# The first 21 of 98 destination blocks of a graph network leave the dense count matrices and take row gathers with one-hot products

## The reference

```python
deg_out = segment_sum(ones, src, N); deg_in = segment_sum(ones, dst, N)
dout, din = maximum(deg_out, 1) ** -0.5, maximum(deg_in, 1) ** -0.5
def conv(x, W, b):                       # run twice, with W1, b1 and W2, b2
    m = (x * dout[:, None])[src]         # one row for each edge
    return segment_sum(m, dst, N) * din[:, None] @ W + b
```

## Time and profile before

| | |
|---|---|
| median of 3 runs | 7861.12 us (7858.62 to 7862.42) |
| the profiled execution | 7861.93 us, its span 7859.9 us |
| counting stage | from 64 to 1264 us |
| first convolution over counts | 1300 to 2441 us |
| second convolution over counts | 2514 to 3638 us |
| edge stage | from 3779 us to the end |
| busy over the span | PE 88%, DVE 62%, ACT 49%, POOL 42% |

### The profile page before, as it was taken

One profiled execution on the slowest core, in us unless ns is written; L12 is line 12 of the kernel. 1 busy time (PEld: TensorE's weight loads), 2 busy tenths in 40 slices (PEclk: granted clock), 3 DMA queues, 4 the chain that ended last, 5 costly groups with the idle time before them and its releaser, 6 DMA issues.

```text
span 7859.9 us, 124589 instructions
## 1 busy us (share of the span) xinstructions
PE 6932.2 (88%) x37774; PEld 5697.3 (72%) x37775; DVE 4864.2 (62%) x9083; ACT 3889.0 (49%) x7386; POOL 3320.6 (42%) x3464
## 2 busy tenths in 40 slices
PE   6999996999997999998788888888888888888887
PEld 4666664888886788886677777777777777777776
DVE  9999996333333333334666666666666666666665
ACT  6999995666664666665322222222222222222222
POOL 2111110000001000001577777777777777777775
PEclk9999998999998999999877787777777777777777
DMA  4666666555554555555433333333333333333332
GB/s 89 137 139 139 141 139 156 153 145 145 145 145 127 152 145 145 145 145 146 125 86 84 88 84 87 86 84 87 86 86 86 87 85 88 84 87 86 84 88 60
DMA packets 624603, 884.18 MB, mean 112 GB/s; under 512 B 198493, under 2 KB 512316, under 8 KB 618064
## 3 DMA queue, kind: packets, MB, share of 16 engines
q1 hardware_dynamic: 483980, 490.53, 21.9%
q0 software_dynamic: 114320, 377.25, 20.5%
q10 hardware_dynamic: 26036, 12.80, 0.6%
HBM read 684.41 MB, written 195.81 MB: 112 GB/s over the span
## 4 chain that ended last, share of the span: by engine, by line
POOL 33%; issue 12%; DMA 3%; DVE 2%; POOLq 1%; DVEq 1%; SPq 0%; PE 0%; ACT 0%; ACTq 0%
POOL t_rows L1566 33%; DMA t_rows<-table,t_ends 2%; DMA t_attrs<-in_edge_attr 1%; DVE t_msg_ad L1780 1%; DVE t_msg_bc L1794 0%; POOLq L173 0%; DVE t_cg L1779 0%; SPq L1538 0%; DVE t_msg_ad L1782 0%; POOLq L1564 0%; DVE t_ge L1776 0%; DVE t_rel L1867 0%; DVE acc L1757 0%; DVE t_msg_bc L1789 0%; DVEq L1878 0%
## 5 line engine op out<-in xcount | busy, mean ns | idle before, releaser
L1566 POOL DMA_INDIRECT t_rows<-table,t_ends x3224 | 3048.4, 946 | 1008.6 <-issue 966.2
L1587 ACT ACTIVATE t_weight<-t_weight,t_attrs 128x64 f32<-128x64 f32 x3224 | 691.9, 302 | 2662.3 <-PE t_weight L1666 2628.2
L937 ACT ACTIVATE c_wide_act<-c_raw 128x1024 fp32r<-128x1024 uint8 (+1 forms) x1400 | 1457.4, 1043 | 648.6 <-PE c_sums L1011 641.5
L1702 PEld LDWEIGHTS t_sums<-t_hot,t_msg_ad 128*128 128x128 f32 x6464 | 969.3, 235 | 916.9 <-issue 916.4
L992 DVE CAST c_wide_dve<-c_raw 128x1024 fp32r<-128x1024 uint8 (+1 forms) x1400 | 770.6, 552 | 1353.8 <-PE c_sums L1011 1353.2
L1011 PE MATMUL c_sums<-c_wide_act,c_parts 128*128 128x512 f32 (+1 forms) x5600 | 1485.1, 387 | 70.1 <-DVE c_parts L976 60.9
L1702 PE MATMUL t_sums<-t_hot,t_msg_ad 128*128 x6464 | 1000.2, 321 | 615.9 <-DVE t_hot L1874 615.5
L1011 PEld LDWEIGHTS c_sums<-c_wide_act,c_parts 128*128 128x128 f32 x5600 | 1044.2, 189 | 290.6 <-issue 80.5
L1011 PE MATMUL c_sums<-c_wide_dve,c_parts 128*128 128x512 f32 (+1 forms) x4200 | 1169.1, 387 | 0.0
L705 ACT ACTIVATE a_a_sb<-a_sums 128x784 bf16<-128x784 f32 x1568 | 1140.6, 941 | 25.2 <-PE a_sums L672 24.7
L1776 DVE TENSOR_TENSOR t_ge<-t_rows,t_edge 128x768 f32<-128x768 f32 x403 | 384.4, 954 | 1204.3 <-DMA t_rows<-table,t_ends 1191.0
(11 more groups left out here) (203 smaller groups left out, 5225.9 us busy)
## 6 DMA issues: line engine op xcount, KB each, us to landing
c_raw<-a_dram SPq DMA_DIRECT2D x672, 448.0 KB, 3.4
a_dram<-a_a_sb POOLq DMA_DIRECT2D x49, 3136.0 KB, 18.2
t_scal<-in_edge_attr SPq DMA_DIRECT2D x403, 256.0 KB
t_rows<-table,t_ends POOLq DMA_INDIRECT x3224
t_ends<-in_edges SPq DMA_DIRECT2D x403, 8.0 KB
t_attrs<-in_edge_attr SPq DMA_DIRECT2D x403, 16.0 KB
c_raw<-a_dram SPq DMA_DIRECT2D x28, 224.0 KB, 2.5
table<-n_out SPq DMA_DIRECT2D x24, 256.0 KB, 2.3
```

Source lines behind the costliest of these rows:

```text
L937: act.activation(to, of, ACT.Copy).then_inc(act_wide, 1)
L1566: pool.indirect_dma_start(out=rows[:, slot, t, :], out_offset=None, in_=table, in_offset=bass.IndirectOffsetOnAxis(ap=ends[:, slot, t:t + ...
L1587: mul = act.activation(ad, ad, ACT.Copy, scale=attrs[:, slot, t, 0:1])
L1702: pe.matmul(sums[:, of, 0:WIDE], msg_ad[:, slot % 2, t, :], hot[:, of, t, :], start=t == 0, stop=t == T - 1)
```

## The change

The destinations of the first 21 blocks (nodes 0 to 2687, FIRST = 21, SPARSE = 2688) belong to the first SG = 88 groups of edges. They are no longer counted into dense matrices.

- In the counting stage 39 pairs are left of 49 (77 blocks, the last pair half empty). For the 21 blocks only the in degree is counted: their edges are still gathered, 11 times two gathers, and compared on DVE (`thin_pair`). Their share of the out degree comes from one-hot products of the source indices of the 88 groups (`make_source_hot` on DVE, `sum_sources` on PE), spread over the batches 3, 5 and 7 of the pairs. `take_first`, once, prepares indices and relative destinations of the 88 groups.
- In each of the two convolutions over counts 20 spans are left of 25, the last with half the columns. In the same steps POOL gathers the rows of the 88 groups (8 gathers each, two buffers), DVE makes a one-hot of 64 destinations, PE multiplies after every third step (8 fp32 matmuls of 64 columns), and DVE adds the result to the accumulator. Gathers start when `parts` is complete, since their buffer overlays the one through which the features came.
- The table of group bounds is no longer kept in SBUF from the start; each fallback stage and the edge stage load it.

The core of the diff (renamed arguments, allocations of tiles and semaphores left out):

```diff
-PAIRS = NB // 2
+FIRST = 3 * OWN
+SPARSE = FIRST * P
+SG = 88
+EDGE = SPARSE - SLOT
+PAIRS = -(-(NB - FIRST) // 2)
+THIN = -(-FIRST // 2)
+STEPS_OF_N = 3
...
+        def source_groups(m, n):
+            some = range(SG * m // PAIRS, SG * (m + 1) // PAIRS)
+            return some[n // 2 - 1:n // 2] if n in (3, 5, 7) else ()
...
                 for m in range(PAIRS):
+                    if m < THIN:
+                        gather(thin_place(m), [block_of(m, h, 0, FIRST) for h in range(2)])
                     if m + STAGED < PAIRS:
-                        gather(m + STAGED)
+                        gather(place(m + STAGED), [block_of(m + STAGED, h) for h in range(2)])
...
+                def thin_pair(m):
+                    at = thin_place(m)
+                    dve.wait_ge(staged_landed[at % STAGED], 32 * (at // STAGED + 1))
+                    for h in range(2):
+                        g = block_of(m, h, 0, FIRST)
+                        last = dve.tensor_tensor(thin_hit[:, h], staged[:, at % STAGED, h, :, 1],
+                                                 own[:, g:g + 1].to_broadcast([P, SLOT]), ALU.is_equal)
+                    last.then_inc(taken, 1)
+                    dve.wait_ge(taken, at + 1)
+                    for h in range(2):
+                        g = block_of(m, h, 0, FIRST)
+                        last = dve.tensor_reduce(degree[:, g:g + 1], thin_hit[:, h], AX.X, ALU.add)
...
+                def take_first():       # 9 operations on [P, 704], 2 on [P, 704, 2], 2 small ones
...
+                def make_source_hot(q):
+                    if q >= 2:
+                        dve.wait_ge(src_summed, q - 1)
+                    some = slice(q * T, (q + 1) * T)
+                    for hot, tab, of, cols in ((src_lo_hot, lo_tab, src_lo, P), (src_hi_hot, key_tab, src_hi, HI)):
+                        halves = [P, T, cols // 2, 2]
+                        last = dve.tensor_tensor(
+                            hot[:, q % 2].rearrange("p s (l k) -> p s l k", k=2),
+                            tab[:, 0:cols].rearrange("p (l k) -> p l k", k=2)[:, None].to_broadcast(halves),
+                            of[:, some, None, :].to_broadcast(halves), ALU.is_equal)
...
                         make_hot(m * (P // BATCH) + n)
                         if n == 1 and m + 2 < PAIRS:
                             split_pair(m + 2)
+                        if n == 2 and 1 <= m <= THIN:
+                            thin_pair(m - 1)
+                        if n == 2 and m == 0:
+                            take_first()
+                        for q in source_groups(m, n):
+                            make_source_hot(q)
...
+                def sum_sources(q):
+                    pe.wait_ge(src_hot_ready, q + 1)
+                    for t in range(T):
+                        mm = pe.matmul(over_src, src_lo_hot[:, q % 2, t], src_hi_hot[:, q % 2, t],
+                                       start=False, stop=False)
...                                                        # convolve_counts
+            @block.gpsimd
+            def _(pool):
+                pool.wait_ge(part1, NHC)
+                pool.wait_ge(part0, NHC)
+                if scaled is not None:
+                    for i in range(NHC - XSLOTS, NHC):
+                        pool.wait_ge(kept[i % XSLOTS], rows_of_slot(i))
+                for q in range(SG):
+                    if q >= 2:
+                        pool.wait_ge(few_ready, q - 1)
+                    for t in range(T):
+                        pool.indirect_dma_start(
+                            out=rows_of_group[:, q % 2, t], out_offset=None, in_=table_of_rows,
+                            in_offset=bass.IndirectOffsetOnAxis(ap=c.first_src[:, q * T + t:q * T + t + 1], axis=0),
+                        ).then_inc(landed[q % 2], 16)
...
                 dve.memset(flat[:, NB * P:(NB + 1) * P], 0.0)
+                dve.memset(flat[:, 0:SPARSE], 0.0)
+                def make_few_hot(q):
+                    if q >= 1:
+                        dve.wait_ge(few_ready, q)
+                    dve.tensor_tensor(hot, c.iota[:, None, 0:WIDE].to_broadcast([P, T, WIDE]),
+                                      c.first_rel[:, q * T:(q + 1) * T, None].to_broadcast([P, T, WIDE]),
+                                      ALU.is_equal).then_inc(hot_ready, 1)
+                def add_few(q):
+                    if q % T == 0:
+                        dve.load(near, c.first_at[0:1, q:q + T])
+                    there = bass.ds(dve.snap(near[q % T], min_val=0, max_val=EDGE), WIDE)
+                    dve.wait_ge(few_ready, q + 1)
+                    dve.scalar_tensor_tensor(flat[:, there], few[:, 0:WIDE], c.ok[:, 0:1], flat[:, there],
+                                             ALU.mult, ALU.add).then_inc(few_added, 1)
...
+                    q = group_after(n)      # n = 15, 18, 21, ...: q = 0, 1, 2, ...
+                    if q is not None:
+                        make_few_hot(q)
+                        if q >= 1:
+                            add_few(q - 1)
+                add_few(SG - 1)
...
+                def sum_few(q):
+                    pe.wait_ge(landed[q % 2], (q // 2 + 1) * 16 * T)
+                    pe.wait_ge(hot_ready, q + 1)
+                    if q >= 1:
+                        pe.wait_ge(few_added, q)
+                    for t in range(T):
+                        mm = pe.matmul(few[:, 0:WIDE], rows_of_group[:, q % 2, t], hot[:, t],
+                                       start=t == 0, stop=t == T - 1)
+                    mm.then_inc(few_ready, 1)
...
+                        if n >= 1 and group_after(n - 1) is not None:
+                            sum_few(group_after(n - 1))
...                                                        # convolve_rest, and alike in product_edges
+                sp.dma_start(bounds[:], bounds_dram.rearrange("(a g) e -> a (g e)", a=1)).then_inc(bounds_landed, 16)
```

More of the change, by code:

```diff
@@ L177, with __init__ @@
 class Bounds:
-    def __init__(self, engine, name, c):
-        self.engine, self.c = engine, c
+    def __init__(self, engine, name, table):
+        self.engine, self.table = engine, table
         self.pairs = [[engine.alloc_register(f"{name}_{p}{i}") for i in range(4)] for p in "ab"]
     def load(self, g, pair):
-        self.engine.load(self.pairs[pair], self.c.bounds[0:1, bass.ds(g * 2, 4)])
+        self.engine.load(self.pairs[pair], self.table[0:1, bass.ds(g * 2, 4)])
     def load_next(self, g, slot):
@@ L445, in _ @@
                 dve.tensor_copy(first_h[:], first_i[:])
-                dve.tensor_copy(own[:], own_i[:].rearrange("p j k -> p (j k)"))
+                dve.tensor_copy(own[:, 0:NB], own_i[:].rearrange("p j k -> p (j k)"))
+                dve.memset(own[:, NB:NB + 1], -1.0)
                 dve.wait_ge(landed, 16)
@@ L578, in _ @@
                 dve.memset(ones[:], 1.0)
+                dve.memset(over_src, 0.0)
                 dve.tensor_copy(lo_tab[:], c.iota[:])
@@ L638, in _ @@
                 dve.tensor_reduce(c.out_degree[:], over_d[:, 0:HI * UNIT].rearrange("p (h d) -> p h d", d=UNIT),
-                                  AX.X, ALU.add)
+                                  AX.X, ALU.add).then_inc(made, 1)
+                dve.wait_ge(src_summed, SG)
+                dve.wait_ge(made, 4)
+                dve.tensor_tensor(c.out_degree[:], c.out_degree[:], over_src, ALU.add)
             @block.tensor
@@ L678, in _ @@
                         turn(m + 2)
+                    if u % (BATCH // UNIT) == BATCH // UNIT - 1:
+                        for q in source_groups(m, at // (BATCH // UNIT)):
+                            sum_sources(q)
                     if at == UNITS_OF // 2 and m == PAIRS - 1:
-                        pe.wait_ge(total_ready, 1)
+                        pe.wait_ge(total_ready, 2)
                         pe.wait_ge(kept, PAIRS)
-                        pe.matmul(turned[:, 0, 0:1], ones[:], total[:], start=True, stop=True).then_inc(all_ready, 1)
+                        pe.matmul(turned[:, 0, 0:2], ones[:], total[:, 0:2], start=True, stop=True
+                                  ).then_inc(all_ready, 1)
                 for u in range(ALL - LAG, ALL):
@@ L856, in blocks_of, with group_after @@
             return min(2, PAIRS - 2 * span)
+        def group_after(n):
+            q, rest = divmod(n - NHC - 1, STEPS_OF_N)
+            return q if rest == 0 and 0 <= q < SG else None
+        table_of_rows = table if scaled is None else scaled
+        assert NHC + 2 + (SG - 1) * STEPS_OF_N < NSPAN * NHC
         def widen(n, unit):
@@ L1078, in _ @@
                     dve.reg_add(rels, rels, 1)
-                    dve.load([first, past], c.bounds[0:1, bass.ds(g * 2, 2)])
+                    dve.load([first, past], bounds[0:1, bass.ds(g * 2, 2)])
                     with dve.Fori(first, past, WIDE) as at:
@@ L1100, in _ @@
                 pe.reg_mov(visits, 1)
```

(3 more changed lines are left out.)

193 lines of the change are left out of this document (140 added, 53 removed).

## The result

The median of the changed kernel is 7636.7 us (7632.5 to 7641.6) against 7861.2 for the one before, a ratio of 0.9715 [0.9698, 0.9732]: 224 us saved, 15 less than the 7652 forecast, and inside the range of 7460 to 7760. A second run of the same file gave 7637.8 and 0.9711 [0.9695, 0.9727].

The account below looks back on a forecast made before the run. DVE was to bound counting and POOL, slowed by casts holding its gathers, the convolutions. From 7861.9 us: -148 counting, -31 and -34 convolutions, +1.5 and +2 small terms, giving 7652; range 7460 to 7760.

Parts of the forecast that it names:

- The counting stage: One-hot batches of the counting stage: DVE alone bounds them, 1035 us against 1187, with ACT and PE keeping up.
- The 4 us for the clock: Counting stage: 4 us added because PE's clock falls while PE stands during `take_first` and comes back a little late.
- Small terms: Outside the main stages: +1.5 us for loading bounds in fallback and edge stages, +2 for the extra tail operations.
- The five spans: Each convolution, PE's side: five spans go at 44.4 us each, -222 us.
- POOL's side: Convolutions: casts hold gathers, a group takes POOL 11.5 us, so POOL ends them, -31 and -34 us.
- The rhythm of two gathers in 3.17 us: Convolutions: gathers released by one cast run into the next, locking two gathers to 3.17 us, 12.0 a group.
- PE's product: Convolutions: a group's 8 fp32 matmuls of 64 columns cost PE 1.0 us with waits, +88 us each convolution.
- PE idle before its 64-column products: Sign expected in the convolutions' trace: PE waits before these products, released by the rows' DMA.
- the rival in which the casts don't hold: Convolutions: gathers stay at 944 ns, PE stays the bound, both gain 126 us: 7465 us, chance 0.14.
- G = 10.8: Convolutions: POOL's time for a group if gathers meet casts at random (drifting); gains 92 and 95 us, 7530 in all.
- The rival that `make_few_hot` holds too: Convolutions: `make_few_hot`, reading bf16, also holds gathers, 0.17 us a group, 30 in all: 7682 us, chance 0.07.
- PE's clock: Rival in the convolutions: PE standing 1 us in 11.5 lowers its clock to 0.85, 12.4 us a group: 7812, chance 0.07.

Follow-up runs that it names:

- experiment 7: Changed kernel without the row gathers, `make_few_hot`, the 64-column products and `add_few` in the convolutions, so 20 spans run alone: 7263.9 us, ratio 0.9238.
- Experiment 2: Changed kernel with PE multiplying only 4 of the 8 row tiles of each group, gathers untouched: 7619.0 us, ratio 0.9687.
- experiment 4: Changed kernel with POOL gathering only 4 of 8 row tiles of a group and PE using each twice: 7591.6 us, ratio 0.9651.
- experiment 1: Changed kernel with DVE's widening casts in the convolutions written as tensor_reduce over an axis of length one, same values: 7613.0 us, ratio 0.9677.
- experiment 3: Changed kernel with tensor_reduce in place of DVE's casts and only 4 of 8 products of each group: 7478.5 us, ratio 0.9509.
- experiment 6: On experiment 1: relative destinations copied to an fp32 tile, so `make_few_hot` has no bf16 operand: 7606.8 us, ratio 0.9673.

## Why the prediction was right, and which term was not

- **The counting stage** was forecast at 1035 us on DVE and took 1032.8. A source pair costs 0.60 + 0.48 = 1.08 us from start to start (1.07 forecast). `take_first` took 89.50 - 81.55 = 7.95 us instead of 10: its tensor_scalar operations and casts of 704 elements take 0.44 from start to start, the tensor_tensor ones 0.9. DVE alone bounds the stage, as forecast; ACT was forecast at 92% and is at 90.8%. The 4 us for the clock didn't come: it is 1.00 in the window. That is most of the 6 us by which the term was off.
- **Small terms**: +3.5 forecast, +1.1 found.
- **The five spans** were priced at 222 us, and experiment 7 measured 221 and 225.
- **POOL's side** came out as forecast, the last digit by luck. The first gather starts at 1236.4 (forecast 0.8 after the end of `parts` at 1235.7), a group takes 11.51 and 11.43 us against the 11.5 chosen, and 1236.4 + 88 x 11.51 + 6.3 = 2255.6 is the end that the trace has at 2255.1. The casts do hold. But 11.5 had been chosen between 10.8 and 12.0 without a sum, and the trace makes up its 11.5 from other parts (mean over both convolutions): 10.0 without holds, 1.06 for holds by casts as forecast, 0.06 for holds by `make_few_hot`, 0.21 for gathers held a second time, and 0.14 for pauses of POOL (beyond the usual 0.3 us). The last two (see the last section) were not in the forecast. The rhythm of two gathers in 3.17 us that the forecast described is there too, though not for long: this stretch of POOL has starts at 1376.61 and 1379.78.

```profile
1376.61 1.39 POOL L1021 DMA_INDIRECT c_early<-table,c_first_src  x1 [0.30 <-issue]
1378.31 1.17 POOL L1021 DMA_INDIRECT c_early<-table,c_first_src  x1 [0.30 <-issue]
1379.78 1.39 POOL L1021 DMA_INDIRECT c_early<-table,c_first_src  x1 [0.31 <-issue]
```

- **The mis-sized term is PE's product**: "16 of them take 3830.99 - 3829.26 = 1.73 us ... so 0.87, and 1.0 with the waits". The "x16" in the earlier trace rows counts records, and an fp32 matmul leaves two. The edge stage's program shows it: that line is run 8 times for a group, once more where a group's destinations need a second window of 64, and the page counts 6464 records, 404 x 8 x 2. Experiment 2 shows it too: 4 products leave 8 records. So 1.73 us was the time of 8 products, and a group costs PE 1.8 us. For 88 groups that is 158 us instead of 88. PE's gain in a convolution was never 126 but 222 - 158 - 8 = 56; with POOL out of it (experiment 4) the first convolution takes 1080.4 us, a gain of 60.
- This error did no harm to the forecast itself, since POOL is still the slower by 0.2 us a group, and both convolutions ended within 3 us of it. It spoilt two other things. What the profile was to show, "PE idle before its 64-column products", came 66 times in 176 groups, 44 us in all. And the rival in which the casts don't hold, given 7465 with a chance of 0.14, was wrong in its price: built as experiment 1, it takes 7613. Only with the product at half its length too (experiment 3) does it come to the 7478 that the rival had meant. The low end of the range rested on that price. The forecast's own low end, 7530 for G = 10.8, has the same flaw: with a group of 11.3 on PE, any G below that leaves PE to set the end, and experiment 1, with POOL at 10.3, takes 7613. So all of the range below some 7600 went by the wrong price.
- **The rival that `make_few_hot` holds too** was true and small: 121 gathers are held by it alone in the changed kernel, 11 us together over both convolutions, against 30 priced. In the forecast the 11.5 happened to contain it.
- **The rule of the Trainium skill** on the hold (page "SBUF — State Buffer", section "Who interferes with whom") is borne out for casts: 643 gathers end 0.81 us after the end of one (see the last section). The same section says that `tensor_reduce` never contends; experiment 1 agrees, with 3 of 1408 gathers over 959 ns beside no `make_few_hot`, the longest 1.01 us. For a tensor_tensor with two SBUF inputs the section tells of contention with GpSimd's reads, and infers that descriptor generation isn't stopped, so it doesn't settle the case of a gather. The runs do: with one bf16 operand 160 of the 162 gathers that it covered were held, with fp32 alone 20 of 159, and of 227 that the edge stage's own one-hot, also fp32, covered in the kernel before none lasted over 0.96 us. Why 20 are still held with fp32 operands isn't shown, nor whether the type itself or another property of the operand decides.
- **PE's clock**, a rival at 7812, stayed at 0.99 in both steady windows, where PE stood for 1.2% of the time. In experiment 2 it stood for 5% (929.73 of 979 us busy from 1236 to 2215) and the clock was 0.99 too, so standing of this size didn't lower it. The edge stage stays at 0.78.

The fastest version that computes everything is that of experiments 1 and 6, 24 to 31 us below the changed kernel. Beyond it PE's products are the limit: half of them gone took 135 us off experiment 1 (7613.0 to 7478.5), until POOL is level with PE again.

## What to carry to other kernels

Before a duration is divided by a count of a trace, the count is checked against the loop in the program: records are not instructions. When the costs of two engines for one unit of work come out within a few per cent of each other, both have to be priced to that accuracy, since the smaller decides what every improvement of the larger is worth (24 and 18 us alone, 158 together). Work put on an idle engine is to be priced beside its new neighbours: the same gather is 944 ns in one stage and 1110 in another.

## What the hardware showed that was not expected

- **A gather can be held twice.** The one at 1705.17 above took 1.65 us. The `make_few_hot` beside it ended at 1705.71, 0.54 after its start, which explains only some 0.4 of its extra 0.7 us. It ends at 1706.82, 0.12 after the cast that ran from 1706.01 to 1706.70:

```profile
1706.01 0.69 DVE L1174 CAST c_wide_dve<-c_raw 128x1024 fp32r<-128x1024 uint8 x1
```

  In the changed kernel 921 gathers last over 959 ns, together 233 us over 944 ns each. Of these 643 (186 us) end 0.81 us after a cast's end, 121 (11 us) end 0.81 us after that of a `make_few_hot`, and 155 (36 us), the longest 1.73 us, end 0.12 us after a cast's end; 2 fit none of these. In experiment 1, where DVE makes no casts beside the gathers, none is of the third kind. That a gather touches the shared resource a second time, 0.12 us before its end, fits these; no run tried it alone.
- **Casts are lengthened too.** Those of 1024 elements take 0.69 us alone and up to 0.95 beside gathers, most of the long ones when they start 0.6 us after a gather's start (108 of 119 over 0.75 us); the mean of all casts on DVE is 585 ns, against 552 before.
- **POOL makes a pause of mostly 2 to 3 us after the 113th gather of a convolution and every 112 from there**, six in each, 15 and 13 us together. It is at the same places in experiments 1, 2, 3 and 6, and never in the edge stage, where the gathers stand in a loop (POOL is never idle for more than 0.32 us between two of them). The first of them:

```profile
1396.73 1.02 POOL L1021 DMA_INDIRECT c_early<-table,c_first_src  x1 [0.30 <-issue]
1400.65 0.94 POOL L1021 DMA_INDIRECT c_early<-table,c_first_src  x1 [2.90 <-issue]
```

  Nothing in the trace releases it, and eleven of the twelve overlap with no transfer of instructions. Its cause is open. Its 15 us are 0.17 of the 11.51 us of a group in the first convolution.
